# A graph network's edge pass: one addition over gathered rows made in two halves, with older work between them

## The reference, cut to what matters

```python
msg_s = (s_n @ Ws_src)[src] + (s_n @ Ws_dst)[dst]
msg_v = einsum('ncx,cd->ndx', v_n, Wv_src)[src] + einsum('ncx,cd->ndx', v_n, Wv_dst)[dst]
m1_s, m1_v = cg_tp(msg_s, msg_v, y0, y1, w1...)     # products with the edge's direction and radial weights
val_s, val_v = linear and gates of m1
m2_s, m2_v = cg_tp(val_s, val_v, y0, y1, w2...)     # a second such product
h = linear of m2, per head                          # stored, and later summed by dst with softmax weights
...
```

## Time and profile before

| what | value |
|---|---|
| median of 3 runs | 7651.65 us (7642.49 to 7712.88) |
| the profiled execution | 7652.89 us, span 7650.8 us |
| mean granted TensorE clock | 0.963 of full speed |
| TensorE busy (matmul) | 6740.5 us, 88% |
| VectorE busy | 6774.3 us, 89% |
| ScalarE busy | 5152.1 us, 67% |
| GpSimd busy | 5186.6 us, 68% |
| message additions | 392, 825 ns each |
| gathers of the first edge pass | 3136, 3085.2 us together |

### The profile page before, as it was taken

How to read it: one execution, slowest core, us unless ns; L and a number is a source line. 1 busy time by engine, 2 the same in 40 slices (tenths; PEclk the granted TensorE clock), 3 DMA queues, 4 the chain that set the end, 5 groups by cost and what they waited for, 6 DMA issues and landing times. The chain is left out here.

```text
span 7650.8 us, 192788 instructions
## 1 busy us (share of the span) xinstructions
PE 6740.5 (88%) x44602; PEld 5311.3 (69%) x44603; DVE 6774.3 (89%) x15045; ACT 5152.1 (67%) x16654; POOL 5186.6 (68%) x5264
## 2 busy tenths in 40 slices
PE   7588998888888888898888849999788999999996
PEld 4488888877787777787878739986444455555556
DVE  8599999999999999999999888877678889999997
ACT  3377777777777777777777611126677888888884
POOL 3477777777777777777777639840677777776650
PEclk7699999999999999999999969989999999999998
DMA  6454444434334343343343337773445555555546
GB/s 207 122 109 107 109 109 108 107 107 106 106 109 108 107 108 106 108 107 108 106 108 107 94 104 248 218 141 106 121 131 133 136 140 141 142 138 137 135 121 193
DMA packets 971090, 967.48 MB, mean 126 GB/s; under 512 B 452030, under 2 KB 788030, under 8 KB 970942
## 3 DMA queue, kind: packets, MB, share of 16 engines
q0 software_dynamic: 225792, 385.65, 21.3%
q1 hardware_dynamic: 511312, 346.34, 16.5%
q10 hardware_dynamic: 233936, 234.90, 9.2%
HBM read 677.51 MB, written 288.65 MB: 126 GB/s over the span
## 5 line engine op out<-in xcount | busy, mean ns | idle before, releaser
L720 POOL DMA_INDIRECT e_g_src<-table_src,e_idx x1568 | 1593.0, 1016 | 504.8 <-issue 477.6
L1907 POOL DMA_INDIRECT f_e<-table,f_src x1568 | 1491.5, 951 | 540.0 <-issue 441.9
L720 POOL DMA_INDIRECT e_g_dst<-table_dst,e_idx x1568 | 1492.2, 952 | 477.9 <-issue 371.2
L757 PE MATMUL e_ps_t<-ident,e_m 128*128 128x128 f32 (+1 forms) x7840 | 1154.4, 278 | 433.0 <-DVE e_m L977 427.1
L1965 PE MATMUL f_ps_a<-f_q,f_onehot 128*128 128x384 f32 x3936 | 1407.2, 501 | 1.9 <-DVE f_q L2055 1.9
L757 PEld LDWEIGHTS e_ps_t<-ident,e_m 128*128 128x128 f32 (+1 forms) x7840 | 864.3, 139 | 558.1 <-issue 499.8
L1965 PEld LDWEIGHTS f_ps_a<-f_q,f_onehot 128*128 128x128 f32 x3936 | 710.1, 190 | 507.6 <-issue 101.5
L850 ACT ACTIVATE e_m1t<-e_ps_t 128x512 f32<-128x512 f32 (+1 forms) x1176 | 693.8, 596 | 371.7 <-PE e_ps_t L757 245.9
L783 PE MATMUL e_ps_v<-e_w_v,e_m1t 128*128 128x64 f32 x3136 | 651.5, 290 | 0.0
L814 PE MATMUL e_ps_h<-e_w_h,e_m2t 96*128 96x96 f32 x3136 | 650.2, 289 | 0.0
L813 PEld LDWEIGHTS e_ps_h<-e_w_h,e_m2t 128*128 128x128 f32 x3136 | 508.7, 192 | 191.0 <-issue 188.9
(11 more groups left out here) (265 smaller groups left out, 16798.6 us busy)
## 6 DMA issues: line engine op xcount, KB each, us to landing
edge_values<-e_h ACTq DMA_DIRECT2D x392, 330.0 KB
r_h<-edge_values SPq DMA_DIRECT2D x196, 660.0 KB, 4.0
sums<-f_acc ACTq DMA_DIRECT2D x492, 192.0 KB
e_g_src<-table_src,e_idx POOLq DMA_INDIRECT x1568
e_g_dst<-table_dst,e_idx POOLq DMA_INDIRECT x1568
f_e<-table,f_src POOLq DMA_INDIRECT x1568
f_rbf<-basis SPq DMA_DIRECT2D x492, 48.0 KB
basis<-t_part SPq DMA_DIRECT2D x42, 448.0 KB, 3.1
```

Source lines behind the costliest of these rows:

```text
L720: pool.indirect_dma_start(out=into[:, r, t, :], out_offset=None, in_=table, in_offset=bass.IndirectOffsetOnAxis(ap=idx[:, r, c:c + 1], axi ...
L757: last = nc.tensor.transpose(ps_t[bank][0:channels, t * P:(t + 1) * P], rows(t), ident[:])
L1907: pool.indirect_dma_start(out=rows_of_units[:, place * T + t, :], out_offset=None, in_=table, in_offset=bass.IndirectOffsetOnAxis(ap=src[: ...
```

## The change: what it does

The message addition becomes two instructions of two tiles each, 320 elements on each lane. `message` keeps the waits and adds the tiles 0 and 1. The new `rest_of_message` adds the tiles 2 and 3, without a wait of its own. Between the two stand the dot of two and the cross of two of group u-2; the dot of three and the third cross of that group come behind the second half. Since each group now has one more step in the count `first`, its length goes from 11 to 12 and the positions move by one; MSG, at which the message is complete, is 2, and GpSimd waits for that before it refills a slot.

```diff
--- before.py
+++ after.py
@@ -629,8 +629,8 @@
         kept = sem("kept")
         leaked = sem("leaked")
         scaled_v = sem("scaled_v")
-        FIRST, SECOND, THIRD = 11, 9, 2
-        MSG, VY, TURNED, DOT2, DOT3, CROSS3, DONE_S = 1, 2, 3, 4, 5, 7, 9
+        FIRST, SECOND, THIRD = 12, 9, 2
+        MSG, VY, TURNED, DOT2, DOT3, CROSS3, DONE_S = 2, 3, 4, 5, 6, 8, 10
         MIXED, SUMMED, GV, VY_2, TURNED_2, DOT2_2 = 1, 2, 3, 4, 5, 6
         msg_v = msg[:, :, CS:D].rearrange("p t (x c) -> p t x c", x=3)
         m1_pairs = m1[:, :, MID + CS:MID + 2 * P].rearrange("p t (x k c) -> p t x k c", x=3, k=2)
@@ -712,7 +712,7 @@
                 if not present(u):
                     return
                 pool.wait_ge(idx_in[r], (i + 1) * 16)
-                wait(pool, first, (u - RING) * FIRST + 1 if not isinstance(u, int) or u >= RING else 0)
+                wait(pool, first, (u - RING) * FIRST + MSG if not isinstance(u, int) or u >= RING else 0)
                 pool.sem_inc(issued, 1)
                 for side, (table, into) in enumerate(((table_src, g_src), (table_dst, g_dst))):
                     for t in range(T):
@@ -981,7 +981,10 @@
             def message(u, r, i):
                 dve.wait_ge(gathered[r], (i + 1) * 32 * T)
                 wait(dve, first, u * FIRST)
-                add(msg[:], g_src[:, r], g_dst[:, r]).then_inc(first, 1)
+                add(msg[:, 0:2], g_src[:, r, 0:2], g_dst[:, r, 0:2]).then_inc(first, 1)
+
+            def rest_of_message(u, r):
+                add(msg[:, 2:4], g_src[:, r, 2:4], g_dst[:, r, 2:4]).then_inc(first, 1)
 
             def products_with_y(u):
                 dve.wait_ge(weighted, u + 1)
@@ -1091,6 +1094,7 @@
                 message(u, r, i)
                 second_dot_of_two(w)
                 second_cross_of_two(w)
+                rest_of_message(u, r)
                 second_dot_of_three(w)
                 second_cross_of_third(w)
                 products_with_y(u)
```

## The result

| | before | changed |
|---|---|---|
| median of 7 runs each | 7672.41 us (7642.49 to 7712.88) | 7604.62 us (7591.12 to 7620.85) |
| profiled execution | 7652.89 us, span 7650.8 | 7612.34 us, span 7610.2 |

The ratio of the runs is 0.9913, 95% interval 0.9885 to 0.9942: 0.9% less time. Taken from the ratio that is 67 us, with an interval of 44 to 88 us. The forecast was 7608 us and 44 us less; the profiled executions differ by 40.6.

What follows compares the result with a forecast made beforehand. GpSimd's issuing of gathers was taken to bound the first edge pass. The hold falling from 0.289 to 0.177 us in 392 groups gives 44 us: 7652.9 - 44 = 7609, against the median 7608; 8-in-10 range 7570 to 7665.

Steps and rivals of the forecast that it cites:

- The bound: First edge pass: GpSimd's issuing of gathers sets the 10.31 us a group, 10.02 plus 0.29 of hold; VectorE needs only 9.79.
- The rule of the hold: A gather starting over some 0.03 us into a two-SBUF-operand VectorE instruction is held until that instruction's end minus 0.13 us.
- The halves: Message addition as two 320-element instructions of 0.48 us each, costing VectorE 0.06 us more a group, 24 us over the pass.
- The sum: Hold over 392 groups of the first edge pass falls from 0.289 to 0.177 us each, 44 us gained.
- Rival 1 and 4: Hold only moves to the next gather, or is a fixed stall per message; 7652 plus or minus 10 us; together 0.14.
- Rival 3: A gather in progress holds the second half, about 0.32 us more of VectorE a group; +35 us, 7687 us; chance 0.05.
- Rival 2: Hold nearly vanishes as gathers fall between shorter instructions once the phase shifts; 76 to 112 us less, 7540 to 7575; chance 0.07.
- The cover: VectorE's 0.52 us wait a group for gathers hides the halves' extra 0.06 us; without it the whole +24 us would count.
- theory D: From the experiments: VectorE's wait for landings places its addition where a gather falls into it; without the wait the hold falls.

Runs made afterwards that it cites:

- halves_together: Changed kernel with the two halves directly behind each other and the four older steps after them; ratio 0.9946, pass 47 us less than before.
- whole_after_two: Kernel before with the undivided addition moved behind the dot of two and the cross of two; ratio 1.002, pass 8 us more than before.
- whole_late_2: Kernel before with the undivided addition moved behind dot of two, cross of two and dot of three; ratio 0.9989, pass 7 us less.
- three_and_one: Changed kernel with the addition as three tiles and one, placed later, around the third cross; ratio 0.9871, pass 111.6 us less than before.
- extra_256: Kernel before with one more 256-element VectorE product a group, result never read; ratio 0.989, pass 89 us less.
- late_halves: Changed kernel with two equal halves placed later, after the dot of three and around the third cross; ratio 0.985, median 7538.95 us against 7653.22 before.
- after_extra_192: Changed kernel with one more 192-element product a group, result never read, on the chip with the lower TensorE clock; ratio 0.9991.
- quarters: Addition in four one-tile pieces with older steps between them, on the chip with the lower TensorE clock; ratio 1.0024.

## Why the prediction was right, point by point

- **The bound.** GpSimd's issuing, 10.02 us a group plus the hold. Shown: the pass shortened by what the gathers' busy time fell by (48.9 and 48.7 us), and 0.20 us more of VectorE's work did not lengthen it.
- **The rule of the hold.** Each gather that starts inside is held until the VectorE instruction's end less 0.13 us. Shown on the two groups above, by the comparison with all gathers, and by halves_together, where the same work stands in the same place as before and only the length of one instruction changed. The Trainium skill ("SBUF — State Buffer", on the two separate sides) describes such a lock between VectorE instructions with two SBUF inputs and GpSimd instructions that read SBUF; the traces agree in this direction, and show that the issue of a gather is held by it.
- **The halves.** 0.485 us each (forecast 0.48), VectorE's need 10.18 - 0.34 = 9.84 us (9.85), its wait 131 us (130 to 150).
- **The sum.** 0.289 to 0.177 us a group was forecast, 44 us. The pass gave 49 and 44 us in two pairs of profiles. The first comparison of run times, 67 us, holds the forecast only at the edge of its interval; the scatter found in the middle part, which the prediction did not know, is large enough for the rest, but that it made it is not shown for those runs.
- **Some luck in the size.** The sum takes the gathers' places behind the addition's start as unchanged. The same way of adding up was low by 0.08 and 0.04 us a group (31 and 17 us) in whole_after_two and whole_late_2, and far too high in three_and_one. The mechanism was right; that the size came out within 5 us is better than the method can promise.
- **Rival 1 and 4** (the hold moves or is of fixed length): refuted by the busy time. **Rival 3** (a gather in progress holds the second half): the longest half took 0.561 us against a median of 0.485, so a gather pushes it by at most 0.08 us, not by 0.32. By the same place in the Trainium skill the instruction that starts first keeps out the other, whichever it is. Here that and the measurement differ, and the measurement decides: a gather that already runs does not block VectorE for its length.
- **Rival 2** was dismissed for a wrong reason. "The phase is set by the landing, not free" is true only while VectorE waits. extra_256, three_and_one and late_halves leave that state and come within 27 us of the floor of 3924 us (392 times 10.01).
- **The cover.** That the 0.06 us more are hidden behind the wait was right, but the wait was treated as mere slack. It is also what places the addition so that the third gather falls into it.

**Why late_halves doesn't wait.** By the forecast's terms VectorE's steps would add up to 9.79 + 0.06 + 0.11 = 9.96 us a group there, under GpSimd's 10.01, so that it should catch up with the landings. The trace shows what is missing. From 400 to 4200 us VectorE waits for no landing, and a group takes 10.02 us. The two halves cost 0.43 and 0.51 us from start to start, 0.20 more together than the whole addition before. The dot of two of group u, which starts together with a gather in nearly every group, costs 0.04 more (0.248 instead of 0.203). The mean of all dots of two, before and in late_halves:

```profile
L978 DVE TENSOR_TENSOR e_dsum<-e_vy 128x128 f32<-128x128 f32 x784 | 222.4, 284 | 0.0
```

```profile
L978 DVE TENSOR_TENSOR e_dsum<-e_vy 128x128 f32<-128x128 f32 x784 | 237.9, 303 | 4.1 <-DMA e_g_dst<-table_dst,e_idx 3.9
```

With the 9.78 us that VectorE's steps take in the kernel before when the waits are left out, that makes 9.78 + 0.20 + 0.04, some 10.02 us. VectorE's need and GpSimd's, 10.01 with the little hold that is left, meet.

**What stays open.** Since the two needs are so near to each other in late_halves and three_and_one, no run tells the share of the raised need from that of the late place with a divided addition. The runs of after_extra_192 and quarters, which would have tested theory D on the changed kernel, fell on the chip with the lower clock. An addition with an operand in PSUM was not tried; it should hold nothing, as in the trace of before 1445 gathers start well inside an instruction with a PSUM operand and are on average not held at all (0.001 us).

## What to carry to other kernels

When one engine issues indirect DMAs back to back, add up its gaps as well as its busy time before calling another engine the bound, and compare the mean of one issue with its median: here the difference was time in which VectorE held it. A long VectorE instruction with two SBUF operands can cost such an engine nearly its own length (0.65 of 0.82 us here), so divide it, or keep it out of the place where the waits put it. A wait also decides where in the other engine's cycle the next instruction starts. Where the slack is small, as here, filling it with a little work gained more (89 us) than the division did (49 and 44).

## What the runs showed of the hardware

- A gather that starts 0.03 us or more inside a VectorE instruction with two SBUF operands is held for up to 0.65 us (maximum 1.60 us against a median of 0.949). One that starts first does not block that instruction: where both start together it is longer by at most 0.08 us (0.561 against a median of 0.485).
- One more VectorE instruction of 0.41 us in each group made the run 1.1% shorter (extra_256, ratio 0.989).
- TensorE's granted clock in one part of 280 us varied between 0.62 and 0.83 in four profiles of the same work, and was 0.75 to 0.77 over whole runs on one chip, where the kernel before took a median of 12026 us.
